# A graph kernel on one core: the adjacency product by Strassen's seven products on pairs of tiles, attention in a ring of four chunks

## The reference

```
deg = max(sum(A, axis=1), 1)
x1  = layernorm(x + relu((D^-1/2 (A + I) D^-1/2 x + x) @ W0 + b0))
s_a = A @ x1
attn_a = sigmoid([s_a, x1] @ Wa.T + ba);  attn_b = sigmoid([s_a, x1] @ Wb.T + bb)
h   = x1 @ W_sa;  s = h @ a_left[:, None] + h @ a_right[None, :]
e   = where(A != 0, exp(-leaky_relu(s, 0.01)), 0)
x_a = (e / (sum(e, axis=1) + 1e-5)) @ h
x_b = A @ (x1 @ W_gcnb) + b_gcnb
out = layernorm(x1 + sigmoid(attn_a * x_a + attn_b * x_b))
```

## Time and profile before

| | |
|---|---|
| median of 3 runs | 917.06 us (913.9 to 917.07) |
| the profiled execution's own time | 915.05 us |
| its span, first to last instruction | 913.3 us |
| TensorE busy | 885.1 us, 97% |
| VectorE, ScalarE, GpSimd busy | 576.5, 538.3, 89.2 us |
| mean granted TensorE clock | 0.989 of 2.4 GHz |

### The profile page before, as it was taken

One profiled execution on the slowest core, in us unless ns is written; L12 is line 12 of the kernel. 1 busy time (PEld: TensorE's weight loads), 2 busy tenths in 40 slices (PEclk: granted clock), 3 DMA queues, 4 the chain that ended last, 5 costly groups with the idle time before them and its releaser, 6 DMA issues.

```text
span 913.3 us, 20470 instructions
## 1 busy us (share of the span) xinstructions
PE 885.1 (97%) x7829; PEld 781.7 (86%) x7829; DVE 576.5 (63%) x973; ACT 538.3 (59%) x1100; POOL 89.2 (10%) x139
## 2 busy tenths in 40 slices
PE   8978999999999998999999999999999999999996
PEld 6757888888888886887888888888888888888885
DVE  6776554554555437669868667576586586585562
ACT  5744455555555229847867566676585584584640
POOL 1023122212212100000000000000000000000000
PEclk9989999999999998999999999999999999999999
DMA  9969898988998300102120120120120120120000
GB/s 321 314 211 358 300 364 290 351 324 292 349 322 285 122 18 13 53 8 81 65 75 25 52 75 11 63 75 11 63 75 11 63 75 11 63 72 14 13 24 12
DMA packets 63015, 121.64 MB, mean 133 GB/s; under 512 B 6480, under 2 KB 25968, under 8 KB 58864
## 3 DMA queue, kind: packets, MB, share of 16 engines
q1 hardware_dynamic: 58352, 116.69, 36.7%
q10 hardware_dynamic: 4608, 4.20, 1.4%
HBM read 95.69 MB, written 25.18 MB: 132 GB/s over the span
## 4 chain that ended last, share of the span: by engine, by line
PE 80%; ACT 6%; DVE 5%; issue 4%; DMA 3%; SPq 1%; POOL 1%; DVEq 0%; ACTq 0%; POOLq 0%
PE ps L1155 32%; PE ps L1042 22%; PE ps L1118 20%; PE ps L1077 5%; ACT ec L518 3%; DMA strip<-in_adj_dram 2%; ACT em L525 2%; DMA xs<-in_x_dram 1%; DVE em L887 1%; PE ps L1062 1%; POOL wsum L345 0%; PE ps L1025 0%; DVE ec L879 0%; DVE codes L621 0%; DVE y L661 0%
## 5 line engine op out<-in xcount | busy, mean ns | idle before, releaser
L1155 PE MATMUL ps<-fb,em 128*128 128x257 f16 x3072 | 343.0, 274 | 6.1 <-DVE em L887 6.1
L1155 PEld LDWEIGHTS ps<-fb,em 128*128 128x128 f16 x3072 | 301.6, 98 | 45.2 <-issue 6.6
L1042 PE MATMUL ps<-y,codes 128*128 128x257 f16 x2048 | 240.2, 275 | 3.4 <-DVE y L661 3.4
L1118 PE MATMUL ps<-fa,pan 128*128 128x258 f16 x2048 | 228.6, 273 | 0.0
L1042 PEld LDWEIGHTS ps<-y,codes 128*128 128x128 fp8e4 x2048 | 201.6, 98 | 31.4 <-DVE y L661 3.8
L1118 PEld LDWEIGHTS ps<-fa,pan 128*128 128x128 fp8e4 x2048 | 200.4, 98 | 24.9
L518 ACT ACTIVATE ec<-slb,nsb 128x256 f32<-128x256 f32 x512 | 210.9, 494 | 2.2 <-issue 1.3
L879 DVE SCALAR_TENSOR_TENSOR ec<-ec,pan 128x2048 f32<-128x2048 f32 x64 | 146.6, 2291 | 40.5 <-ACT ec L518 40.5
L887 DVE SCALAR_TENSOR_TENSOR em<-ec,em 128x2048 f16<-128x2048 f32 x64 | 146.2, 2284 | 8.4 <-ACT em L525 8.4
L525 ACT ACTIVATE em<-ec 128x2048 f16<-128x2048 f32 x64 | 121.4, 1899 | 10.4 <-DVE ec L879 10.4
L549 ACT ACTIVATE sg<-w 128x256 f32<-128x256 f32 x32 | 13.3, 417 | 167.0 <-DVE w L914 167.0
(11 more groups left out here) (99 smaller groups left out, 498.7 us busy)
## 6 DMA issues: line engine op xcount, KB each, us to landing
strip<-in_adj_dram SPq DMA_DIRECT2D x128, 512.0 KB, 6.4
a_scratch<-codes SPq DMA_DIRECT2D x16, 1024.0 KB, 9.6
pan<-a_scratch SPq DMA_DIRECT2D x16, 1024.0 KB, 5.1
x_scratch<-x ACTq DMA_DIRECT2D x32, 128.0 KB, 4.6
x1r<-x_scratch SPq DMA_DIRECT2D x32, 128.0 KB, 2.0
out_dram<-ot SPq DMA_DIRECT2D x32, 128.0 KB, 1.7
xs<-in_x_dram SPq DMA_DIRECT2D x3, 1024.0 KB, 10.3
slb<-sl_scratch SPq DMA_DIRECT2D x16, 128.0 KB, 4.8
```

The costliest lines, as they stand in the source:

```text
L1042: mm = pe.matmul(ACC(n), codes[:, qq % SLOTS, h, jb, e * P:(e + 1) * P].bitcast(F8), y[:, jb, part, 0:YC], start=(jb == 0 and part == 0), ...
L1118: mm = pe.matmul(PA(b)[:, 0:GC], pan[:, slot, jb, (b % 2) * P:(b % 2 + 1) * P].bitcast(F8), fa[:, jb, part, 0:GC], start=(jb == 0 and part ...
L1155: mm = pe.matmul(PH(b)[:, 0:HC], em[slot][:, e_part, jb, (b % 2) * P:(b % 2 + 1) * P], fb[:, jb, h_part, 0:HC], start=(jb == 0 and e_part ...
```

## The change

A tile pair p of rows and the two column tiles of a panel make a 2 x 2 block of A, X11, X21, X12, X22. The product of each block with g, whose columns are also cut into two halves, is written in Strassen's form: seven products M1 to M7 of a 128 x 128 matrix (X11, X22, or one of five differences of blocks) with a form of g (a half, or a sum or difference of halves). Each form is stored as high and low part side by side, so one matmul of 260 columns (M2 to M5, with the columns of Wa and Wb) or 256 columns (M1, M6, M7) does both parts. A panel takes 7 x 16 = 112 matmuls in place of 128.

- **Differences** of the codes are made by DVE, five instructions per panel, each on 128 x 512 words of 32 bits.
- **Forms** of g are made in stage 2 for each pair of tiles: POOL's `g_sums` (three instructions), ACT's high parts (three), DVE's `forms_lo` (three); `g_lo` goes.
- **Accumulators**: M3 and M5 use bank 0, M4 and M2 bank 1, M1 and M7 bank 2, M6 bank 3. M2 and M5 can only begin when DVE's `middle` has read M3 and M4, M7 when `middle_m1` has read M1, and the next panel's M3 only when `combine` has read banks 0 to 3. ACT copies low parts out first (`low_m34`, `low_m1`, `low_all`).
- **Attention chunks**: `em` is one ring of four chunks. TensorE does a chunk (48 matmuls) and then two products of the next panel, four times; a chunk's buffer is written again once TensorE has read it.
- **h** is written by ACT's queue to DRAM tile by tile (except for the last two), and loaded in four transfers when A y is finished, since `fb` now lies where y was.
- **Epilogue** for both tiles of a panel at once: the bias is added by POOL (`pool_bias`, 128 x 512), the final normalization is ACT's (`norm`), POOL also makes the shift, the store is one transfer per panel.

The diff, cut to its core:

```diff
+PROD = ("M3", "M4", "M1", "M6", "M2", "M5", "M7")
+        def g_sums(eng, p):
+            eng.wait_ge(S["g_ready"], 2 * p + 2)
+            eng.tensor_tensor(gb[:, 2, :], gb[:, 0, :], gb[:, 1, :], ALU.add)
+            eng.tensor_tensor(fs[:, 0, :], gb[:, 0, H1], gb[:, 1, H2], ALU.subtract)
+            eng.tensor_tensor(fs[:, 1:3, :], gb[:, 0:2, H1], gb[:, 0:2, H2], ALU.add).then_inc(S["gsum_ready"], 1)
...
@@ proj_copies (ACT, stage 2)
+                if 0 < n < T - 1:
+                    act.wait_ge(S["hlo_ready"], n)
+                    act.dma_start(hd[:, n - 1, :], hst[:, (n - 1) % 2].rearrange("p k c -> p (k c)")
...
-                act.activation(fa[:, t, 0, 0:GC], BG(n)[:, 0:GC], ACT.Copy, scale=1.0 / PROJ
+                act.activation(gb[:, n % 2, :], BG(n)[:, 0:GC], ACT.Copy, scale=GSC).then_inc(S["g_ready"], 1)
...
+                if n % 2:
+                    act.wait_ge(S["gsum_ready"], p + 1)
+                    act.activation(fa4[:, p, 0:2, 0:P + 2], gb[:, 0:3:2, 0:P + 2], ACT.Copy)
+                    act.activation(fa4[:, p, 2:4, 0:P + 2], gb[:, 1:3, P:GC], ACT.Copy)
+                    act.activation(zz[:, p, 0:3 * D].rearrange("p (a b) -> p a b", b=D)[:, :, 0:P], fs[:], ACT.Copy
+                                   ).then_inc(S["ghi_ready"], 1)
...
@@ ACT, stage 3
+            def low_all(u):
+                gate(act, S["prod_done"], u * NPROD + NPROD, "passed_act")
+                gate(act, S["mid_read"], u * 2 + 2, "passed_act")
+                act.copy(lc[:, 0:2, :], ps[:, 0:2, P + 2:2 * P + 4])
+                act.copy(lc[:, 2:4, 0:P], ps[:, 2:4, P:2 * P]).then_inc(S["low_all"], 1)
+            def act_step(s, m, nth, first=False, second=False):
+                if not first:
+                    low_all(s)
+                high_chunk(s, 3, first)
                 exp_chunk(s + 1, n, 0, nth)
+                gates(s, m)
                 exp_chunk(s + 1, n, 1)
+                high_chunk(s + 1, 0)
+                if not first:
+                    sigmoid(s - 1)
+                low_m34(s + 1)
+                gated(s, m, first)
                 exp_chunk(s + 1, n, 2)
+                high_chunk(s + 1, 1)
+                low_m1(s + 1)
+                if not first:
+                    norm(s - 1, second)
                 exp_chunk(s + 1, n, 3)
+                high_chunk(s + 1, 2)
...
@@ DVE
+            def difference(slot, op, p0=0, p1=NP):
+                o, a, b = differences(slot, op, p0, p1)
+                return dve.scalar_tensor_tensor(out=o, in0=b, scalar=0x7f7f7f7f, in1=a, op0=ALU.bitwise_and,
+                                                op1=ALU.bitwise_xor)
+            def middle(u):
+                gate(dve, S["low_m34"], u + 1, "passed_dve")
+                dve.tensor_tensor(m34[:], ps[:, 0:2, 0:P + 2], lc[:, 0:2, :], ALU.add).then_inc(S["mid_read"], 1)
+                gate(dve, S["mid_read"], u * 2 + 1, "passed_dve")
+                st.then(dve.tensor_tensor(t134[:], halves(m34)[:, 0, :], halves(m34)[:, 1, :], ALU.add))
+            def combine(u, first=False):
+                wq = w[:].rearrange("p e (h c) -> p (e h) c", c=P)
+                gate(dve, S["low_all"], u + 1, "passed_dve")
+                st.then(dve.tensor_tensor(s52[:], ps[:, 0:2, 0:P + 2], lc[:, 0:2, :], ALU.add))
+                dve.tensor_tensor(s67[:], ps[:, 2:4, 0:P], lc[:, 2:4, 0:P], ALU.add).then_inc(S["acc_read"], 1)
...
+            def dve_step(s, m, nth, second=False):
+                combine(s)
+                low_chunk(s, 3)
+                all_differences(s + 1, n)
                 mask_chunk(s + 1, n, 0)
+                attend(s - 1, n, second)
+                low_chunk(s + 1, 0)
                 mask_chunk(s + 1, n, 1)
+                middle(s + 1)
+                statistics(s - 1)
+                low_chunk(s + 1, 1)
                 mask_chunk(s + 1, n, 2)
+                middle_m1(s + 1)
+                low_chunk(s + 1, 2)
                 mask_chunk(s + 1, n, 3)
+            middle(0)
             row_factors()
+            middle_m1(0)
+            mask_chunk(0, 0, 0)
...
+            combine(0, first=True)
+            mask_chunk(0, 0, 1)
+            low_chunk(0, 0)
+            mask_chunk(0, 0, 2)
+            low_chunk(0, 1)
+            dve.wait_ge(panel_in[1], 16)
+            all_differences(1, 1)
+            mask_chunk(0, 0, 3)
+            low_chunk(0, 2)
+            denominators()
+            low_chunk(0, 3)
+            mask_chunk(1, 1, 0)
+            low_chunk(1, 0)
+            mask_chunk(1, 1, 1)
+            middle(1)
...
@@ PE
+            def product(slot, name, p0=0, p1=NP):
...
+                    if name in ("M2", "M3", "M4", "M5"):
+                        g, c = fa4[:, p, side, 0:2 * P + 4], P + 2
+                    else:
+                        g, c = zz[:, p, side * D:(side + 1) * D], P
+                    mm = pe.matmul(ps[:, bank, 0:2 * c], a.bitcast(F8), g, start=(p == 0), stop=(p == NP - 1))
+            def pe_step(s, m, nth):
+                e_chunk(s, m, 0)
+                free_products(s, m, nth)
+                e_chunk(s, m, 1)
+                outer_products(s, m)
+                e_chunk(s, m, 2)
+                onto_products(s, m)
+                e_chunk(s, m, 3)
+                last_product(s, m)
```

More of the change, by code:

```diff
@@ L595, in _ @@
-            for e in range(2):
-                sigmoid(e, e)
-            act_panel(1, 1, 2)
-            with act.Fori(1, NQ - 1) as k:
-                act_panel(k * 2, 0, k + 1)
-                act_panel(k * 2 + 1, 1, k + 2)
-            act_panel(NPAN - 2, 0, NQ)
-            for e in range(2):
-                gates(T - 2 + e, 1, e)
-                gated(T - 2 + e, e)
-            for e in range(2):
-                sigmoid(T - 2 + e, e)
+            exp_chunk(0, 0, 0, first=True, behind={4: low_m34})
@@ new lines, in _ @@
+            low_m1(0)
+            act.wait_ge(S["acc_done"], T)
+            for j in range(SLOTS):
+                act.wait_ge(codes_out[j], 32 * len(range(j, NQ, SLOTS)))
+            high_chunk(0, 0, True)
+            exp_chunk(0, 0, 1, first=True, behind={2: low_all})
+            act.wait_ge(S["arg_ready"], 1)
+            act.activation(rr[:], tb[:], ACT.Exp).then_inc(S["rr_ready"], 1)
+            exp_chunk(0, 0, 2, first=True)
+            high_chunk(0, 1, True)
+            for j in range(X1RING):
+                act.wait_ge(x1_out[j], 16 * T // X1RING)
@@ new lines, in _ @@
+            act.wait_ge(S["proj_done"], T)
+            exp_chunk(0, 0, 3, first=True)
+            high_chunk(0, 2, True)
+            act_step(0, 0, 1, first=True)
+            act_step(1, 1, 2, second=True)
+            act_step(2, 0, 2)
+            with act.Fori(1, NPAN // 2 - 1) as k:
+                act_step(k * 2 + 1, 1, k + 2)
+                act_step(k * 2 + 2, 0, k + 2)
+            low_all(NPAN - 1)
+            high_chunk(NPAN - 1, 3)
+            gates(NPAN - 1, 1)
+            sigmoid(NPAN - 2)
@@ L846, in _ @@
             dve.tensor_scalar(slb[:], slb[:], sc[:, NMAX], None, ALU.min).then_inc(S["slb_ready"], 1)
+            forms_lo(NP - 1)
+            for op in range(NDIFF):
+                difference(0, op, NP - 2, NP).then_inc(S["diff_ready"], 1)
             def row_factors():
@@ new lines, in statistics @@
+            def statistics(s):
+                gate(dve, S["sigmoid_ready"], s + 1, "passed_dve")
+                gate(dve, x1r_in, s * 16 + 16, "passed_dve")
+                dve.scalar_tensor_tensor(out=sg[:], in0=sg[:], scalar=0.5, in1=x1r[:], op0=ALU.mult, op1=ALU.add
+                                         ).then_inc(S["x1r_used"], 1)
+                gate(dve, S["x1r_used"], s + 1, "passed_dve")
+                for e in range(2):
+                    st.then(dve.bn_stats(two(BN2, 6)[:, e, :], sg[:, e, :]))
@@ new lines, in _ @@
+            mask_chunk(1, 1, 2)
+            middle_m1(1)
+            low_chunk(1, 2)
+            mask_chunk(1, 1, 3)
+            dve_step(1, 1, 2, second=True)
+            dve_step(2, 0, 2)
+            n0, per_pair = st.n, 2 * 12
+            with dve.Fori(1, NPAN // 2 - 1) as k:
+                st.n, st.base = n0, k * per_pair - per_pair
+                dve_step(k * 2 + 1, 1, k + 2)
+                dve_step(k * 2 + 2, 0, k + 2)
+                assert st.n - n0 == per_pair, st.n - n0
@@ L1000, in _ @@
+            st.n, st.base = n0 + (NPAN // 2 - 2) * per_pair, 0
+            combine(NPAN - 1)
+            low_chunk(NPAN - 1, 3)
+            attend(NPAN - 2, 0)
+            statistics(NPAN - 2)
+            attend(NPAN - 1, 1)
+            statistics(NPAN - 1)
         @block.tensor
@@ L1185, in _ @@
[L1185 to L1196 removed]
+            pe.wait_ge(S["forms_ready"], NP)
```

616 lines of the change are left out of this document (336 added, 280 removed).

## The result

The change made the kernel slower: 942.78 us against 915.93 for before in the same runs, a ratio of 1.030, 95% interval [1.029, 1.032], where 905 was forecast. The profiled execution took 943.04 us, its span is 941.2.

A forecast was written before the change was run, and what follows sets the result against it. TensorE's matmuls were taken as the bound. Terms -28.2 + 1.5 + 13.2 + 0 + 3.1 = -10.4 us took the profiled 915.05 to about 904.7, or 906.7 by the runs' median; forecast 905, range 894 to 916.

The forecast's parts named there:

- What bounds the kernel, and what is removed: Whole kernel: TensorE's matmuls are the bound; A g goes from 2048 to 1792 matmuls at 110 ns, 28.2 us less.
- the ring: Panels: DVE and ACT waiting for each other, mask, high, low and exps; 32.3 us a step, under TensorE's 33.4.
- Stage 2: Stage 2: extra forms work is hidden except at the entry, where p_step(2) comes 1.5 us later; bounds 0 and 3.
- Into stage 3: Beginning of stage 3: four TensorE waits and clock losses, less the 8.6 us lost before: +13.2 us, bounds +5 and +20.
- All four waits: TensorE's waits at the beginning of stage 3, 5.2, 4.1, 2.7 and 6.9 us, sum 18.9.
- waits 1 and 4: Stage 3's beginning, before panel 0's first products and panel 1's M2: 5.2 and 6.9 us; clock falls, costing 0.4 and 2.5.
- wait 2: Stage 3's beginning, after panel 0's M2, M5, M7, until combine's two reads: 4.1 us, with no clock term of its own.
- The panels: Steps of stage 3: TensorE's 33.4 us sets the pace and it never waits: 0 us, the upper end being the ring.
- The slack: Panels: least margin between DVE's results being ready and TensorE asking for them, 3.4 us.
- the one on the other side: Rival: doubled all_differences price makes the ring 35.4 us, 14 x 2.0 less 3.4 slack, +24.6, 929; gain gone from 34.4; 12 in 100.
- Fewer matmuls don't shorten a panel: Rival, panels: 260 columns and changing banks cost 119 ns a matmul, gain 17 us less, 922 us; 1 in 100.
- The end: After the last matmul: both tiles' epilogue stands there, +3.1 us, bounds 2 and 4.5; about 10.7 us to the end.

The follow-up runs named there:

- experiment 1: Changed kernel with ACT's norm moved behind the step's last exp_chunk and high_chunk: 908.79 us, ratio to before 0.993.
- experiment 7: Changed kernel, norm left in place, with one wait added: DVE stands still after statistics until POOL's power and shifts are done; 907.79 us, ratio to before 0.993.
- experiment 6: experiment 1 plus panel 0's chunk 3 before panel 1's M2/M5, last forms and differences before the wait for POOL's reduce, low_m34 after first exp: 903.15 us.
- experiment 2: Changed kernel with POOL's bias add left out, so the bias is missing from the output: 931.23 us, ratio to before 1.018.
- experiment 8: experiment 1 with all five differences of each panel made twice, with a short wait between the rounds: 925.98 us, ratio to before 1.012.
- experiment 5: experiment 1 with POOL's bias add left out as well, so the bias is missing from the output: 907.36 us, ratio to before 0.993.

## Why the prediction was wrong, point by point

- **What bounds the kernel, and what is removed**: right. With the ring out of the way (experiments 1 and 7) a step is 33.46 us against 35.20: 1.74 x 16 = 27.8 us, forecast 28.2. Strassen's products run at 110 ns (32 in some 3.5 us), banks and widths cost nothing.
- **Stage 2**: right; `p_step(2)` started at 98.60, the forecast's time to the digit, and its links held (sums to 95.8 for 95.7, high parts to 96.95 for 96.9, low parts to 98.2 for 98.1).
- **Into stage 3**: 16.8 us where 13.2 were forecast, within its bounds. All four waits came in their places (5.74, 2.29, 0.61, 7.76 us for 5.2, 4.1, 2.7, 6.9); with 1.13 ahead of the transpose they sum to 17.5 us, forecast 18.9. M2 of panel 0 started at 350.48, forecast 346.1 + 1.5 = 347.6. The row for it is POOL's reduce: its input was ready at 342.57, it started at 346.54, behind 9.42 us in which the profile shows nothing that it waited for, and the last forms and differences stood behind it on DVE. The forecast had no term for it; in the kernel before, the same reduce had started 0.13 us after its input (343.20). This counts as the reason in part only: experiment 6 took the forms and differences from behind it and won 1.0 us. The clock fell behind waits 1 and 4 as forecast (32 matmuls in 5.65 and 6.35 us, at granted clocks of 0.63 and 0.55), and it was low again behind wait 2, of 2.29 us, where the sum had nothing: M3 and M4 of panel 1 took 5.37 us at 0.68. How the 3.6 us divide between the late reduce and the low clock is not shown.
- **The panels**: this is the step that failed. "Then ACT, which waited for POOL's shift and normalized, ends its exps at 25.8", 5.7 us after `statistics` at 20.1, has in it, besides the exps and the normalization (3.3 and 1.1), POOL's power and shifts at the durations that they have alone (some 1.2 us). Measured, from the end of statistics (718.95) to that of the exps (728.44), it is 9.5 us: POOL 4.9 in place of 1.2. The ring of 32.3 became 36.4, over TensorE's 33.4. The slack was used up in the first two steps, and 35.3 us are lost in all: 14 steps of 36.36 for 33.45 would be 40.7, so the slack was worth some 6 us, where 3.4 were forecast. The bias add took its part: 0.8 us a step in the mean (experiment 2), where the prediction had 1.4 us as a case and a price of 1 us, because on a ring of 32.3 it first had to use up the slack; on one that is the pace already it counts from the first step.
- **The rule was at hand, and applied at one of two places.** The Trainium skill ("SBUF — State Buffer", Who interferes with whom) says that a DVE instruction with two SBUF inputs contends with a GpSimd instruction that reads SBUF. The prediction used it for the bias add, in which DVE is the one to suffer, and not for the power and the shifts, which stand behind `statistics` right beside `low_chunk` and `mask_chunk`. By rows of the trace: the power overlaps `low_chunk` for 2.06 us and ends 0.57 us later. The trace agrees with the rule, and the cost falls on the side that the prediction didn't ask about. The trace of before had the warning too, and not only in the cast of 0.69 that took 1.28. The same kind of power, on one element, stood behind `stats` in stage 2 and took 1.16 us in the median, up to 1.21; in stage 3 it took 0.55. Its page, and its timeline where DVE's casts run beside it:

```profile
L375 POOL TENSOR_TENSOR sc<-sc,sc 128x1 f32<-128x1 f32 x32 | 17.7, 555 | 549.0 <-DVE sc L930 484.9
...
L363 POOL TENSOR_TENSOR lnst<-lnst,sc 128x1 f32<-128x1 f32 x32 | 32.8, 1026 | 206.9 <-DVE lnst L790 206.9
```

```profile
282.45 1.29 DVE L621 TENSOR_SCALAR codes<-strip 128x1024 uint8<-128x1024 f32 x2
282.57 1.21 POOL L363 TENSOR_TENSOR lnst<-lnst,sc 128x1 f32<-128x1 f32 x1 [6.56 <-DVE lnst L790]
...
299.75 0.55 POOL L363 TENSOR_TENSOR lnst<-lnst,sc 128x1 f32<-128x1 f32 x1 [6.33 <-DVE lnst L790]
```

  At 282.57 the power ends 0.04 us after DVE's two casts; at 299.75 DVE stands idle and it takes 0.55. The cast has one tensor input, so these rows don't show what `low_chunk` with two would do, but a power that doubles beside 1.29 us of DVE was the question to ask of one placed beside 2.29.
- **The rivals**: the one on the other side had the mechanism right (a ring of DVE and ACT that sets the pace, slower than TensorE) and the place wrong: it put it in `all_differences`, which cost 3.09 us for five as priced. Its formula held: from 34.4 us on the ring costs the gain, and experiment 8's ring of 34.7 gives 926 us, slower than before. For the panels alone the formula gives 14 x 1.3 - 3.4 = 14.8 us; from panel 1's first chunk to the last panel's e h experiment 8 takes 484.0 us, experiment 1 468.4, 15.6 more. For the changed kernel's ring of 36.36 it gives 38.0, for 35.3 measured. "Fewer matmuls don't shorten a panel" is refuted by experiment 1.
- **The end**: 10.4 us for 10.7.

With `norm` moved, the time is within 4 us of the forecast of 905 (908.8); the best version measured is experiment 6 with 903.15 us, 1.2% under before.

## What to carry to other kernels

Where two engines wait for each other in a ring, price each link at the duration that it has beside what runs at that moment, above all a tiny GpSimd instruction that starts inside a long two-input DVE instruction: here it ended some 0.5 us after that one's end. What waits for it belongs behind the work that the ring needs, or the long instruction belongs behind it: a wait of 1.8 us on a busy engine was worth 35 us here. And ask of a small wait what is queued behind it: leaving the bias add out was worth 0.8 us a step while the ring set the pace (experiment 2), and nothing once TensorE did (experiment 5). Last, look for an instruction that has two durations in the trace of before: the power's 0.55 and 1.21 us were there.

## What was not expected of the hardware

- A GpSimd instruction that starts 0.2 us into a 2.29 us `scalar_tensor_tensor` of DVE (both inputs in SBUF, 2048 elements a partition) takes 2.63 us instead of 0.70, and two of one element each take 1.92 instead of 0.50. The other way round, when GpSimd's add of 512 elements starts 0.05 us ahead (737.00), it takes 1.27 us and DVE's instruction 3.37 instead of 2.29. In these pairs the one that starts first is not slowed (DVE's 2.29 us is what it takes elsewhere), and the other waits for nearly all of it. In experiment 1 the add comes second, 0.27 us into `low_chunk`, and takes 3.15 us.
- TensorE's waits of some 2.8 us ahead of M3 were followed by the lower clock (1.2 of 2.4 GHz) in some steps and not in others. The windows of the changed kernel (busy times of PE, PEld, DVE, ACT, POOL, then the granted clock) over M2 and M5 of panel 1 and over M3 and M4 of two panels, the one from 590.48 behind a wait of 2.82 us, the other from 772.30 behind 2.75:

```profile
393.40:399.50 6.10, 6.10 (x32) 4.34 (x33) 4.69 (x4) 4.90 (x10) 0.00 (x0) 0.55 0.00 0
590.50:595.50 5.00, 5.00 (x33) 3.86 (x34) 4.72 (x6) 5.00 (x13) 1.27 (x1) 0.71 0.69 236
771.00:775.00 4.00, 2.70 (x25) 2.42 (x26) 3.72 (x9) 3.64 (x6) 1.27 (x1) 1.00 0.54 172
```

  The slow M3 and M4 took 5.11 us in place of 3.71. While the ring sets the pace that costs nothing: the next wait was 1.34 us, and the M3s stood 36.4 us apart all the same. At the beginning even the wait of 2.29 us (360.16) was followed by 32 matmuls in 5.37 us, while nothing was lost behind the wait of 2.32 us in the kernel before.
- GpSimd's first instruction behind the reduce (L442) started 7 to 8 us after its input, with no releaser in the profile, whatever it was: the first bias add at 368.43 (input at 361.13, "issue" 21.51 us), in experiment 2 the first power at 432.47 (input at 424.62), and in the kernel before its first power at 407.71 (input at 399.70). The reduce itself started 4.0 us after its input in the changed kernel and 0.13 us after it in the kernel before. What GpSimd does in that time no run here tells.
